# Favor attention in four streams, with the features taken from the projections in 32x32 tiles of TensorE

## What is computed

```python
# L=3 layers, N_HEAD=16, dh=8, omega (L, 8, 4), so 8 features for each head
def favor(x, omega):                       # x: (B, S, 16, 8)
    xs = x * dh ** (-0.25)
    u = jnp.einsum('bshd,dm->bshm', xs, omega)
    h = 0.5 * jnp.sum(xs * xs, axis=-1, keepdims=True)
    return jnp.concatenate([jnp.exp(u - h), jnp.exp(-u - h)], axis=-1) * m ** (-0.5)

for l in range(L):
    q, k, v = (out @ W[l] + b[l] for W, b in ((Wq, bq), (Wk, bk), (Wv, bv)))   # by head
    Qf, Kf = favor(q, omega[l]), favor(k, omega[l])
    a = causal_linear_attention(Qf, Kf, v)   # num = q (sum k v), den = q (sum k) + 1e-6
    h = layer_norm(out + a @ Wo[l] + bo[l], ln1)
    y = relu(h @ W1[l] + bf1[l]) @ W2[l] + bf2[l]       # 128 -> 512 -> 128
    out = layer_norm(h + y, ln2)
```

## Time and profile before

| | us |
|---|---|
| three runs | 1825.32, 1832.27, 1837.38 (median 1832.27) |
| profiled execution, span from first to last instruction | 1828.0 |
| PE busy | 1571.7 (86%) |
| DVE busy | 1443.5 (79%) |
| ACT busy | 935.3 (51%) |
| POOL busy | 698.6 (38%) |

### The profile page before, as it was taken

One profiled execution on the slowest core, in us unless ns is written; L12 is line 12 of the kernel. 1 busy time (PEld: TensorE's weight loads), 2 busy tenths in 40 slices (PEclk: granted clock), 3 DMA queues, 4 the chain that ended last, 5 costly groups with the idle time before them and its releaser, 6 DMA issues.

```text
span 1828.0 us, 65037 instructions
## 1 busy us (share of the span) xinstructions
PE 1571.7 (86%) x27934; PEld 1150.5 (63%) x27934; DVE 1443.5 (79%) x3906; ACT 935.3 (51%) x1958; POOL 698.6 (38%) x620
## 2 busy tenths in 40 slices
PE   6777365399969999999999999999999999999853
PEld 4344254399946677776667777666677667777542
DVE  4998566766658888888888888888888988888864
ACT  4887476366524444445544444554444544444373
POOL 0777636345513234215224323423321522431354
PEclk9888655599969999999999999999999999999876
DMA  9730012333200000000000000100000000000437
GB/s 264 145 100 1 21 50 90 97 102 101 83 13 14 3 9 9 15 3 14 15 3 13 16 3 8 20 3 9 9 15 3 14 15 3 11 6 3 109 102 233
DMA packets 88606, 79.69 MB, mean 44 GB/s; under 512 B 22416, under 2 KB 77040, under 8 KB 88064
## 3 DMA queue, kind: packets, MB, share of 16 engines
q1 hardware_dynamic: 70736, 46.17, 9.6%
q0 software_dynamic: 10848, 25.70, 4.9%
q10 hardware_dynamic: 6736, 3.66, 0.7%
HBM read 46.74 MB, written 34.01 MB: 44 GB/s over the span
## 4 chain that ended last, share of the span: by engine, by line
PE 50%; DVE 13%; ACT 4%; issue 2%; DMA 1%; DVEq 1%; POOL 0%; another core or an unknown queue 0%; POOLq 0%; ACTq 0%
PE psum L1965 8%; PE psum L1890 8%; PE psum L1859 4%; PE psum L1868 4%; PE psum L1928 2%; PE psum L1934 2%; PE psum L1882 2%; PE psum L1936 2%; PE psum L1875 2%; PE psum L1937 2%; PE psum L1938 2%; PE psum L1948 2%; PE psum L1847 2%; DVE at_kb L1543 2%; PE psum L1929 2%
## 5 line engine op out<-in xcount | busy, mean ns | idle before, releaser
L1890 PE MATMUL psum<-attn_w,at_qa 128*128 128x128 f32 x1536 | 197.6, 282 | 0.0
L1752 POOL TENSOR_TENSOR at_xres<-at_xn,attn_rows 128x512 f32<-128x512 f32 x32 | 40.9, 1277 | 394.2 <-DVE at_xn L368 394.2
L1965 PE MATMUL psum<-at_vT,attn_w 128*128 128x512 f32 x384 | 180.6, 614 | 6.8 <-ACT at_vT L1697 5.8
L1890 PEld LDWEIGHTS psum<-attn_w,at_qa 128*128 128x128 f32 x1536 | 179.6, 192 | 6.1 <-issue 0.7
L1543 DVE TENSOR_SCALAR at_kb<-at_kf,const 128x512 f32<-128x512 f32 x192 | 178.4, 989 | 0.0
L1757 POOL TENSOR_TENSOR at_xn<-at_sqk,attn_rows 128x512 f32<-128x512 f32 x48 | 63.6, 1326 | 202.8 <-DVE at_sqk L368 202.8
L1549 DVE STREAM_TRANSPOSE at_vb<-at_vT 32x512 uint32<-32x512 uint32 x192 | 134.7, 701 | 1.9
L1669 ACT ACTIVATE at_qa<-at_qf,const 128x512 f32<-128x512 f32 x192 | 127.6, 714 | 1.6
L1713 ACT ACTIVATE at_qa<-psum,attn_bf 128x512 f32<-128x512 f32 x192 | 122.1, 678 | 10.6 <-PE psum L1965 5.4
L1565 DVE TENSOR_TENSOR at_weights<-psum,const 128x1024 f32<-128x1024 f32 x96 | 115.6, 1204 | 11.3 <-PE psum L1859 11.3
L361 ACT ACTIVATE at_rstd<-at_mv,const 128x4 f32<-128x4 f32 x96 | 28.1, 292 | 184.3 <-DVE at_mv L349 184.2
(11 more groups left out here) (308 smaller groups left out, 3884.2 us busy)
## 6 DMA issues: line engine op xcount, KB each, us to landing
ex_rows<-sorted_x SPq DMA_DIRECT2D x71, 129.0 KB
ti_rows<-tile_rows SPq DMA_DIRECT2D x8, 640.0 KB
x<-in_L_attn_x SPq DMA_DIRECT2D x8, 512.0 KB, 7.3
tile_rows<-in_L_attn_x SPq DMA_DIRECT2D x8, 512.0 KB
x<-token_y POOLq DMA_DIRECT2D x8, 512.0 KB
tile_y<-ti_rows SPq DMA_DIRECT2D x16, 192.0 KB
out<-x ACTq DMA_DIRECT2D x12, 256.0 KB
expert_w<-in_L_ffn_w SPq DMA_DIRECT2D x1, 2048.0 KB, 14.2
```

The costliest lines, as they stand in the source:

```text
L1890: last = mm(bank(f.s, 1)[:, c * D:(c + 1) * D], hidden[f.s][:, t, c * P:(c + 1) * P], k.w2[:, f.l, t, :], start=(t == 0 and c == 0), stop= ...
L1965: mm(bank(f.s, c), k.w1[:, f.l, c * P:(c + 1) * P], hT[f.s][:], start=True, stop=True).then_inc(hid_ready, 1)
```

## The change

- Four streams. Job n belongs to stream n mod 4 (`Job`), stream t takes batches 2t and 2t+1, and layer l+1 follows four jobs after layer l. Carries are kept for four streams, and the layer norm's outputs `xn` in four buffers.
- Three jobs in a slot. `Slot` names `a` = job n, `p` = job n-1 (output weights and first norm), `f` = job n-2 (feed-forward and second norm), `then` = job n+1. There are 50 slots where there were 49. `xT`, `vT`, `hT` and `attT` have one buffer each.
- Features. `feature_weights` and its three steps are gone. ACT writes the scaled projections of keys and queries (`ks`, `qs`) and their squares (`sqk`, `sqq`) to the space of `weights`. `head_features` multiplies them by the 32x32 blocks of omega and then of `half`: 16 matmuls of 512 columns on 32x32 tiles, in place of four on the whole array. The query weights are loaded turned by 32 channels, so that the queries of quarter (r+1) mod 4 of the rows go to quarter r of the output.
- `carried` uses the unmasked query features with four diagonal 32x32 tiles for each g: 64 matmuls in place of 32.
- Two of the four masked copies of the key features go from DVE to ACT.
- On DVE the second sum stands ahead of both halves of the causal mask. On PE the two halves of `sums` and those of `scores` stand together, and the next input is transposed ahead of `carried`.
- `expert_part` cuts the last of the experts' result into the same number of parts, in the order of the four streams; the layer of tiles takes batches 0, 2, 4, 6, 1, 3, 5, 7.

```diff
+KEYS_BY_VECTOR, KEYS_BY_SCALAR = (0, 1), (2, 3)
...
+    turned = [(slice(SUB, P), slice(0, P - SUB)), (slice(0, SUB), slice(P - SUB, P))]
+    late += [(k.w4[:, 0, :, to], ins["L1_attn_Wq"].rearrange("l c d -> c l d")[:, :, of]) for to, of in turned]
...
+        class Job:
+            def __init__(self, n):
+                self.n, self.s, self.t, self.l, self.group = n, n % 2, n % STREAMS, n // STREAMS % L, n // (STREAMS * L)
...
+                self.a, self.p, self.f, self.then, self.gone = job(i), job(i - 1), job(i - 2), job(i + 1), job(i - 3)
...
-                        for b in range(HQ):
-                            last = nc.vector.tensor_scalar(kb[s][:, :, b, :], kf[s][:].rearrange("p (j i) -> p j i", i=SUB),
-                                                           cst(k, "mask_b")[:, b:b + 1], None, ALU.mult)
...
+                    for b in KEYS_BY_VECTOR:
+                        last = nc.vector.tensor_scalar(kb[a.s][:, :, b, :], kf[a.s][:].rearrange("p (j i) -> p j i", i=SUB),
...
+                def projected(dst, src, which, l):
+                    nc.scalar.activation(dst, src, ACT.Identity, bias=col(which, l), scale=SCALE).then_inc(kqv_taken, 1)
...
+                    for b in KEYS_BY_SCALAR:
+                        last = nc.scalar.activation(kb[s][:, :, b, :], kf[s][:].rearrange("p (j i) -> p j i", i=SUB), ACT.Copy,
...
+                def head_features(a, table, keys, queries, start):
+                    s = a.s
+                    for r in quads:
+                        o = (r + 1) % 4
+                        mm(bank(s, 2)[quad(r), :], table[quad(r), quad(r)], keys[quad(r), :], start=start, stop=not start, skip_group_check=True)
+                        last = mm(bank(s, 3)[quad(r), :], table[quad(o), quad(o)], queries[quad(o), :], start=start, stop=not start, skip_group_check=True)
+                    return last
...
-                        for h in two:
-                            mm(bank(1 - s, 2 + g // 8)[half_of(h), g % 8 * GW:(g % 8 + 1) * GW], qa[s][half_of(h), g, 2 * h:2 * h + 2, :].rearrange("p a i -> p (a i)"),
-                               state[s][half_of(h), :, g], start=(g % 8 == 0), stop=False, skip_group_check=True)
+                        for r in quads:
+                            mm(bank(1 - s, 2 + g // 8)[quad(r), g % 8 * GW:(g % 8 + 1) * GW], qf[s][quad(r), g * SUB:(g + 1) * SUB],
+                               state[s][quad(r), :, g], start=(g % 8 == 0), stop=False, skip_group_check=True)
...
-                        mm(bank(s, 2), wu[1][:, l, :], xT[s][:], start=True, stop=False)
-                        pe.wait_ge(kq_taken, n * 2 + 1)
-                        mm(bank(s, 2), cst(k, "half"), sqk[s][:], start=False, stop=True).then_inc(feat_ready, 1)
...
+                        pe.wait_ge(kqv_taken, n * 5 + QUERIES_IN)
+                        head_features(a, k.omega[:, l, :], ks[s], qs[s], True)
+                        pe.wait_ge(kqv_taken, n * 5 + QUERIES_SQUARED)
+                        head_features(a, cst(k, "half"), sqk[s], sqq[s], False).then_inc(feat_ready, 1)
```

644 lines of the change are left out of this document (331 added, 313 removed).

## The result

| | kernel before | kernel after |
|---|---|---|
| runs, us | 1825.32 to 1837.38, median 1833.74 (4 runs) | 1938.04 to 1959.69, median 1951.57 (4 runs) |
| span of the profiled execution, us | 1828.0 | 1955.6 |

The ratio of after to before is 1.064, 95% interval [1.0587, 1.0693]: slower, where 1717 us was forecast.

The account below looks back on a forecast made before the run. PE's own work was taken to bound the slot, with DVE close behind; 24.88 to 22.4 us over 47 slots saves 117 us: 1828.0 - 117 - 1 + 3 = 1713 us span, plus 4.3 gives 1717 us, range 1675 to 1795.

Parts of the forecast that it names:

- What bounds the kernel now: Attention slot of 24.88 us: PE's own work bounds it, 24.22 us busy; DVE follows 3 us behind.
- the features: Key and query features on PE: eight 32x32 tiles overlap, 1.8 us instead of 3.44, saving 1.64 us a slot.
- The first rival: Diagonal tiles on one bank take turns: features 6.9 us, carried 4.5 us, total 2067 us; chance 0.12.
- the third: Keys and queries sharing a column of tiles take turns: features stay 3.44 us, slot 24.0 us, total 1793 us; chance 0.07.
- the PE sum: PE's work per attention slot: 24.22 - 1.64 (features) - 0.64 (carried) = 21.94 us; joining L1847 and L1859 costs nothing.
- I am wrong if: Refuting signs: L1863 records 0.43 us apart, carried over 2.3 us, over 1 us ACT wait before scores, clock off 1.00.
- I take 1.6 us: carried on four diagonal 32x32 tiles takes 1.6 us instead of 2.24, saving PE 0.64 us a slot.
- The waits that take over: End of slot: PE 21.9 and DVE 22.0 us with its waits bind together; 0.4 us added, slot 22.4 us.
- the 1.1 named as the risk: DVE's two remaining masked keys, taken at 0.94 us each, might cost up to 1.1 us each, 0.3 us more.
- The waiting at the mask: PE waits for DVE's causal mask ahead of L1899 (weighed), half a microsecond or more in most slots.
- Head and tail: Outside the steady slots: 1 us won at the head, 3 us lost in the tail, which now holds two slots.
- the meeting of PE and DVE: Two in-order engines that meet twice a slot do not fit perfectly: 0.4 us added to the slot.

Follow-up runs that it names:

- e1: Kernel after with only carried put back on two 64x64 tiles (32 matmuls): ratio 1.011 to the kernel before, slot 24.94 us.
- e8: e1 plus DVE normalising a first layer's input behind the state's scan instead of ahead of the masked keys: ratio 0.989 to the kernel before, slot 24.16 us.
- e4: Kernel before with the two halves of scores joined in one piece: ratio 1.024, slot 25.71 us.
- e2: Kernel before with carried alone on four diagonal 32x32 tiles (64 matmuls): ratio 1.053, slot 26.89 us.
- e6: Kernel before with 32 unread one-column 32x32 matmuls (128 instructions) per slot in one piece behind carried: ratio 1.058, slot 27.09 us.
- e7: Kernel before with 32 unread one-column matmuls per slot, eight behind each of four 512-column products: ratio 1.051, slot 26.76 us.
- e9: e2 with the second half of the feed-forward's output product moved from between the scores to behind them: ratio 1.042, slot 26.34 us.
- e13: Kernel before with 512, 1024 and 2048 one-column-matmul instructions behind the keys' product of three slots: pieces took 8.3, 13.5, 28.3 us; run 1893.28 us beside 1823.32.

## Why the prediction was wrong

- **"What bounds the kernel now"** and the features were right. The two tables' 32 records started eight at a time:

```profile
1105.89 0.61 PE L1863 MATMUL psum<-at_weights,omega 32*32 32x512 f32 x1
...
1105.93 0.61 PE L1864 MATMUL psum<-at_weights,omega 32*32 32x512 f32 x1
1106.34 0.59 PE L1863 MATMUL psum<-at_weights,omega 32*32 32x512 f32 x1
...
1107.76 0.66 PE L1980 MATMUL psum<-const,at_vT 128*128 128x128 f32 x4
```

From 1105.89 to 1107.76: 1.87 us, forecast 1.8. The first rival (turns at a bank, 2067 us) and the third (a column's tiles take turns) are out. The Trainium skill's "TensorEngine Tiling (Array Packing)", section Restrictions and Gotchas, has the rule that the prediction weighed: different row tiles cannot use one PSUM bank at the same time. The trace says the contrary for these shapes: four row tiles that write one bank, each to its own 32 partitions, started within 0.04 us. By that rule this part alone would have cost 6.9 us, the estimate of the first rival.

- **The step that failed first** is the PE sum: "L1847 and L1859 stand in one piece now, which I cost at nothing", together with the silent assumption that a small matmul costs its execution wherever it stands. There was no term for the delivery of instructions. The trace of before had the hint: its waits view of 600 to 1600 us has "issue" waits of 5.5 us (14 times) inside L1875 and of 3.4 us (12 times) at L1847, all in small matmuls, and its page counts the instruction packets.

```profile
PE psum L1875 <- issue: 5.5, 14, 0.9
PE psum L1847 <- issue: 3.4, 12, 0.3
```

   The signs named as "I am wrong if" caught it: the clock left 1.00. Its size: 82.5 us of waits in 1000 us, about 37 slots, 2.2 us a slot, and 2 x 0.08 x 1000 = 160 us at half clock, 4.3 us a slot, of which at most half is lost. Together up to 4.4 us, against a miss of 27.24 - 22.4 = 4.8. PE's busy time sets a closer bound for the half clock: it is 1.9 us over the forecast, 0.64 of it `carried`, so some 1.3 us are left for it. The waits for at_state, 25.4 us or 0.7 us a slot, are the third part. By edit and not by wait, 2.3 of the 4.8 us came with the four-tile `carried` and its 128 further instructions (e1), 0.8 us with the place of the input norm (e8). The order costed at nothing has a price too: joining the scores alone cost the kernel before 2.4% (e4), but by a wait for DVE.

- **"I take 1.6 us" for carried** failed as well: 2.24 us, the same as before. The estimate went by L1847's and L1875's rate. L1868's 70 ns per record of a tile stayed 70 ns when the tiles were halved (2.24 us/32), so neither turns at the bank nor the number of weight columns sets it. What does stays open.

- **"The waits that take over"**: the sum of DVE's work per slot was near (20.3 measured, 19.35 forecast), but the place of the pieces was left out. The input norm stood ahead of the masked keys in 15 slots; e1 to e8 puts that at 2.2%. The masked keys cost 104.2/96 = 1.09 us each (in the row below), not 0.95, near the 1.1 named as the risk. The waiting at the mask did not happen.

```profile
L1543 DVE TENSOR_SCALAR at_kb<-at_kf,const 128x512 f32<-128x512 f32 x96 | 104.2, 1125 | 0.0
```

- **Head and tail**: from slot 47's key projection to the end of the span 149.3 us, before 137.0. With the slot's own change of 2.4 us taken off, 10 us were lost, forecast 3. The later traces make it more: the same stretch is 130 to 133 us in e2, e4, e6, e7 and e9, which keep the order of the kernel before, and 145 to 152 us in the seven that have the new one, e8 at 150.3 among them. Slot 1 starts 6.5 us later, where a gain of 1 us was expected; but in the later traces both families start it at 522 to 527 us, so that no gain and no loss of the change shows there. Neither was followed up.

- **The sum of the miss**, in ratios: forecast 1717/1832 = 0.937, measured 1.064. Undoing `carried` gives 5.3 points, the late input norm another 2.2, which leaves 0.989. Of the last 5 points the longer end of the attention is one (some 15 us). The rest is e8's slot, 24.16 us for 22.4: 0.64 us of it is the gain of `carried` that did not come; its issue waits are 39.7 us in 1000, 1.0 us a slot, its waits for at_state 0.4 us. How much of these the half clock (0.98) adds to, and how much lies in the meeting of PE and DVE that was put at 0.4 us, was not separated. A supply limit was not among the rivals, so the one case on the slower side was the wrong one.

## What to carry to other kernels

Count instructions, not only microseconds: where small matmuls stand in one dense piece, write beside each block of 256 instructions how long it executes, and if several in a row are well under 3.6 us, expect PE to stop and its clock to fall. This is a warning and no formula: e4's stretch at some 2.8 us a block hardly stopped, e2's at 2.2 us did. The change that halved a tile here and doubled the matmuls bought nothing and cost about 5%, though the array overlapped them all; the breaks show up inside a product, in the middle of its records, often in the one behind the product that was changed. And when an engine loses a copy from its list, look also at what stands ahead of the piece the others wait for.

## What was not expected of the hardware

- In these kernels PE got its instructions at 3.5 to 3.75 us per 256 when it used them at once (e13), 14 ns an instruction; the breaks ended 2.3 to 2.6 us after the start of the fetch that the trace shows, and no two fetches began less than 3.2 us apart (all traces, 600 to 1600 us).
- With stops of 1 to 2 us every 3.6 us and one-column matmuls between them, PE stayed at half clock for the whole piece (e13, 0.50 from 1458 to 1483 us); in the kernel after the clock fell in a stop of 1.53 us.
- A one-column matmul of float32 on a 32x32 tile costs 20 ns in a dense run (0.63 us for 32) and about 50 ns when a group of eight stands between two 512-column products (0.4 us for eight).
- Eight 32x32 tiles with 512 columns, in two banks, run at once; four diagonal tiles of 36 columns that add up in one bank gain nothing over two of 64x64.
